# First group of a retention and FP4-linear kernel: next body's first k projection brought forward, ring loads from the staging area, second gate's transposes behind q

## The reference, cut to what matters

```python
xn = layernorm(x)                                  # x: (4, 1024, 1024)
q, k, v = heads(xn @ Wq + bq) * hd**-0.5, heads(xn @ Wk + bk), heads(xn @ Wv + bv)
ret = einsum('bhid,bhjd->bhij', q, k) * D          # D[i, j] = exp(decay * (i - j)) for i >= j, else 0
ret = ret / clip(abs(ret.sum(-1)), 1)
g = group_norm(einsum('bhij,bhjd->bhid', ret, v)) * gn_w + gn_b
attn = (silu(xn @ Wg + bg) * g) @ Wo + bo
ffn = fp4_quantized(xn) @ fp4_quantized(weight).T * scale + bias
return x + attn + ffn
```

## Time and profile before

| | before |
|---|---|
| median of 3 runs | 2137.29 us (2134.43 to 2142.41) |
| profiled execution, its time | 2142.48 us |
| its span | 2140.7 us |
| granted TensorE clock, mean | 0.991 |
| PE busy | 2080.3 us, 97% |
| DVE busy | 1541.7 us, 72% |
| ACT busy | 685.9 us, 32% |
| POOL busy | 640.0 us, 30% |

### The profile page before, as it was taken

The page is one execution under the profiler, slowest core; times in us unless marked ns, Lnnn a source line. Parts: engine busy times, 40 slices in busy tenths (PEclk is TensorE's granted clock), DMA queues, the critical chain, the costliest instruction groups (busy, mean ns, idle before and its releaser), DMA issues.

```text
span 2140.7 us, 51098 instructions
## 1 busy us (share of the span) xinstructions
PE 2080.3 (97%) x18098; PEld 1053.5 (49%) x18098; DVE 1541.7 (72%) x4375; ACT 685.9 (32%) x1318; POOL 640.0 (30%) x456
## 2 busy tenths in 40 slices
PE   5988899999999999999999999999999999999999
PEld 3444444455455454555555555454555454555444
DVE  7899898988889877566767556767656767656732
ACT  5756623332223233322323322323322322322300
POOL 1323232332233333223332223233223233223220
PEclk8999999999999999999999999999999999999999
DMA  8878634334343443323333323333323333223343
GB/s 317 282 253 265 218 98 138 108 109 136 100 127 108 137 128 94 102 83 109 124 103 93 103 84 109 122 103 94 103 85 107 122 103 95 103 86 106 122 153 117
DMA packets 181686, 275.61 MB, mean 129 GB/s; under 512 B 117344, under 2 KB 117472, under 8 KB 181344
## 3 DMA queue, kind: packets, MB, share of 16 engines
q1 hardware_dynamic: 181600, 274.48, 39.8%
HBM read 204.18 MB, written 40.89 MB: 114 GB/s over the span
## 4 chain that ended last, share of the span: by engine, by line
PE 86%; DVE 11%; DMA 2%; issue 1%; ACT 0%; SPq 0%; DVEq 0%; ACTq 0%
PE mm L1288 54%; PE mm L1223 10%; PE tp L1223 6%; PE mm L1232 4%; PE tp L1298 3%; PE four L1338 3%; PE four L1351 2%; PE tp L1326 1%; PE four L1311 1%; PE four L1232 1%; PE tp L1251 1%; DVE wo L929 1%; DMA res<-in_w_f 1%; DMA parts<-wo 1%; DVE state L1041 1%
## 5 line engine op out<-in xcount | busy, mean ns | idle before, releaser
L1288 PE MATMUL mm<-xnT,wring 128*128 128x512 f16 x6144 | 1365.8, 381 | 13.8 <-DVE wring L929 6.8
L1288 PEld LDWEIGHTS mm<-xnT,wring 128*128 128x128 f16 x6144 | 598.2, 98 | 710.3 <-issue 25.2
L695 ACT ACTIVATE work<-four,gs 128x64 f32<-128x64 f32 x512 | 158.1, 414 | 554.2 <-DVE gs L1068 554.2
L556 POOL TENSOR_TENSOR yT<-gn,gate 128x512 f32 (+1 forms) x64 | 84.2, 1315 | 800.6 <-ACT gn L706 800.6
L1223 PE MATMUL mm<-wo,yT 128*128 128x512 f16 x960 | 214.1, 380 | 0.1
L1055 DVE BATCH_NORM_STATS2 gst<-four 128x6 f32<-128x64 f32 x512 | 73.5, 216 | 195.0 <-PE four L1351 194.8
L539 POOL TENSOR_TENSOR qparts<-qT,qparts 128x512 f16<-128x512 f32 x64 | 77.0, 1203 | 363.2 <-ACT qT L664 363.1
L539 POOL TENSOR_TENSOR kparts<-kT,kparts 128x512 f16<-128x512 f32 x64 | 84.2, 1316 | 225.1 <-ACT kT L664 225.1
L1223 PEld LDWEIGHTS mm<-wo,yT 128*128 (+1 forms) x960 | 91.0, 98 | 108.3 <-issue 0.2
L1223 PE MATMUL tp<-wo,yT 128*128 128x512 f16 x576 | 128.2, 379 | 0.0
L662 ACT ACTIVATE qparts<-mm,consts,down 128x512 f16<-128x512 f32 x64 | 49.7, 776 | 213.2 <-PE mm L1288 213.2
(11 more groups left out here) (198 smaller groups left out, 2648.8 us busy)
## 6 DMA issues: line engine op xcount, KB each, us to landing
wring<-parts SPq DMA_DIRECT2D x252, 512.0 KB, 3.9
xt<-in_x SPq DMA_DIRECT2D x34, 512.0 KB, 3.6
out<-res SPq DMA_DIRECT2D x32, 512.0 KB, 3.0
parts<-wo SPq DMA_DIRECT2D x28, 512.0 KB, 5.6
res<-in_x SPq DMA_DIRECT2D x28, 512.0 KB, 3.5
ftile<-in_w_f SPq DMA_DIRECT2D x12, 512.0 KB, 4.4
parts<-wring SPq DMA_DIRECT2D x8, 512.0 KB, 6.8
probs<-in_x SPq DMA_DIRECT2D x5, 512.0 KB, 4.6
```

The costliest lines, as they stand in the source:

```text
L556: nc.gpsimd.tensor_tensor(hi, gn[:], gate[:, u], ALU.mult)
L695: last = nc.scalar.activation(work[:, c * P + h * HD:c * P + (h + 1) * HD], ao[h][:, c * VW:c * VW + HD], ACT.Identity, bias=gs[:, 1, g:g ...
L1288: last = MM(mm[n % 2][:], wring[:, n, wj, k, :], xnT[:, parity, xj, k, :], start=(j == 0), stop=(j == 3 * KT - 1))
```

## The change

In the first group only: PE does the k projection of the next body's first pair behind the second scores of this one, and ACT evacuates it there (`project` and `evacuate` have an argument `ahead`). `load_slice` reads the slice from `wo` instead of `parts` in all bodies but the last one's second half, and so waits for `lo_done` instead of `stored`; SP's calls of `load_slice(1, n)` are interleaved with the stores of the next batch, and the square that overwrites a slice of `wo` waits until the ring load has read it (`w_k` and so on). PE's `transpose_g(1, 1)` goes behind the q projection, and ACT's `affine(1, 1)` behind the evacuation of q. DVE does the second half of the quantization behind the first states in bodies 1 to 3, and `find_f_max` of the first tiles behind the second mask.

```diff
--- before.py
+++ after.py
@@ -371,10 +371,12 @@
                     w(f"mm{n % 2}_full", mm_use(u, n))
-                    if (phase, i, u) == (FIRST, 0, 0):
-                        sp.wait_ge(stored[n], 32)
-                        sp.wait_ge(lo_done, 4 + n + 1)
-                        src, dst = wo[:, :, 4 + n, :], wring[:, n].rearrange("p b k x -> p b (k x)")
+                    if phase == FIRST and (i, u) != (CH - 1, 1):
+                        b, c = i + u, 4 * (1 - u) + n
+                        if (i, u) == (0, 0):
+                            sp.wait_ge(stored[n], 32)
+                        sp.wait_ge(lo_done, SLICES * b + c + 1)
+                        src, dst = wo[:, :, c, :], wring[:, n].rearrange("p b k x -> p b (k x)")
                     else:
@@ -444,15 +446,17 @@
                         move_x_parts()
                         load_slice(0, 3)
+                    load_slice(1, 0)
+                    pass_on(i + 1, range(0, 1))
+                    load_slice(1, 1)
+                    pass_on(i + 1, range(1, 2))
                     w("xq_ready", 1)
                     move_x()
                     load_x(1)
-                    pass_on(i + 1, range(0, 2))
-                    load_slice(1, 0)
-                    load_slice(1, 1)
-                    pass_on(i + 1, range(2, 4))
                     load_slice(1, 2)
+                    pass_on(i + 1, range(2, 3))
                     load_slice(1, 3)
+                    pass_on(i + 1, range(3, 4))
                     pass_on(i + 1, range(4, 5))
                     load_fs(F_TILES[i][1])
@@ -617,8 +621,9 @@
                         act.wait_ge(stored[c], 16 * (b if c >= 4 else b + 1))
-                    if b == 1 and c >= 4:
-                        act.wait_ge(s["w_" + MATS[c - 4]], 16)
+                    loads = 2 * b - 1 if c >= 4 else 2 * b - 2
+                    if loads > 0:
+                        act.wait_ge(s["w_" + MATS[c % 4]], 16 * loads)
...
@@ -734,13 +741,15 @@
                 hi = lambda *slices: split_hi(i + 1, slices)
-                evacuate(0, 0)
+                if i == 0:
+                    evacuate(0, 0)
                 evacuate(0, 1)
                 if i:
-                    affine(1, 1)
                     square(i + 1, range(0, 4))
                 x_hi()
                 evacuate(0, 2)
+                if i:
+                    affine(1, 1)
                 copy_v(0)
@@ -760,6 +769,8 @@
                 evacuate(1, 3)
                 affine(0)
+                if i + 1 < CH:
+                    evacuate(0, 0, ahead=1)
                 normalize(1)
@@ -1096,8 +1107,6 @@
                     quantize_half(xt, 0)
-                    if i:
-                        quantize_half(xt, 1)
                     mask_scores(0)
@@ -1106,9 +1115,11 @@
                     scale_batch()
                     states(0)
                     split_lo(i + 1, range(0, 2))
-                    find_f_max(F_TILES[i][0])
+                    if i:
+                        quantize_half(xt, 1)
                     group_norm(0)
                     mask_scores(1)
+                    find_f_max(F_TILES[i][0])
                     split_lo(i + 1, range(2, 3))
                     states(1)
@@ -1354,10 +1366,10 @@
-                project(0, 0)
+                if phase != FIRST or i == 0:
+                    project(0, 0)
...
                 project(0, 1)
-                if phase != FIRST or i:
+                if phase != FIRST:
                     transpose_g(1, 1)
                 project(0, 2)
+                if phase == FIRST and i:
+                    transpose_g(1, 1)
                 transpose_kv(0, "v", vT, 1)
@@ -1388,6 +1403,8 @@
                 scores(1)
                 if phase == FIRST:
+                    if i + 1 < CH:
+                        project(0, 0, ahead=1)
                     state_increments(1)
```

More of the change, by code:

```diff
@@ L649, in pair, with evacuate @@
                     return ds(q * 2 + u, 1)
-                def evacuate(u, n):
+                def evacuate(u, n, ahead=0):
+                    w = waiter(act, phase, i + ahead)
+                    at_pair = ds((q + ahead) * 2 + u, 1)
                     use = mm_use(u, n)
@@ L662, in evacuate @@
                         nc.scalar.activation((kparts, None, qparts)[n][:, 0], mm[0][:], ACT.Identity,
-                                             bias=bias[:, n, pair(u)], scale=down[:, n, pair(u)])
+                                             bias=bias[:, n, at_pair], scale=down[:, n, at_pair])
                     nc.scalar.activation(dst, mm[n % 2][:], ACT.Silu if n == 3 else ACT.Identity,
-                                         bias=bias[:, n, pair(u)], scale=down[:, n, pair(u)])\
+                                         bias=bias[:, n, at_pair], scale=down[:, n, at_pair])\
                       .then_inc(s[f"mm{n % 2}_free"], 1)
@@ L1275, in body, with project @@
                     return
-                def project(u, n):
+                def project(u, n, ahead=0):
+                    w = waiter(pe, phase, i + ahead)
                     use = mm_use(u, n)
-                    if (phase, i, u) == (FIRST, 0, 0):
+                    if (phase, i + ahead, u) == (FIRST, 0, 0):
                         pe.wait_ge(lo_done, n + 1)
```

## The result

| | before | after |
|---|---|---|
| median | 2136.68 us of 4 runs (2134.43 to 2142.41) | 2186.95 us of 4 runs (2186.49 to 2188.52) |
| profiled execution, its span | 2142.48 us, 2140.7 us | 2186.86 us, 2185.1 us |

The change makes the kernel slower: ratio 1.0225, 95% interval 1.0205 to 1.0245. The forecast was 2174 us with a range of 2148 to 2194; the time lies in the range and 13 us above the forecast.

A forecast was written before the change was run, and what follows sets the result against it. DVE's chain was taken to bound the first group's bodies 1 to 3, with PE nearly full. Body losses 2 + 10.9 + 13.6 + 9.9 = 36.4 us on the 2137.3 us median gave 2174 us, range 2148 to 2194.

The forecast's parts named there:

- t: Time within a body, in us after DVE starts that body's layernorm.
- the two holds: ACT, bodies 1 to 3: first, affine waits behind x_hi, ending t = 7.9; second, square 7 awaits gate-slice load, t = 24.9.
- only the first hold: Rival: gate slice lands before ACT reaches square 7, so only late affine costs; 2150 us, chance 0.12.
- not slower: Rival: PE, not DVE, is late at a body's head, so late affine delays no one; 2124 us, chance 0.07.
- worse: Rival: gate slice takes twice as long and PE's clock falls in both pauses; about 2191 us, chance 0.09.
- the 4.2 taken: Ring's gate slice load on SP: lands 4.2 us after issue, at t = 24.9; the row used was an HBM load.
- the sum of 36.4: First group's added time over bodies 0 to 3: 2 + 10.9 + 13.6 + 9.9 = 36.4 us.
- without the 1.11 us wait: DVE, end of body 2: FFN weight tile priced at 1.2 us, its earlier 1.11 us wait taken as gone.
- The moved half, priced at 5.0: DVE, bodies 1 to 3: second quantize half behind the first states takes 5.0 us, delaying the first group norm.
- The projection behind the second pause: PE's second v projection after 7.4 us idling: 7.03 us instead of 5.3, bounds 5.3 and 8.6.
- DVE has the last word: First group, bodies 1 to 3: both engines nearly full, DVE sets the pace; a microsecond on its chain is worth a microsecond.
- PE's wait of 2.90 us: Body 2 before: PE stands 2.90 us before state increments until DVE masks the scores; counted as waiting the change removes.

The follow-up runs named there:

- Undoing the two holds: Changed kernel with affine(1, 1) and transpose_g(1, 1) put back and the ring's gate slot load ahead of the transposes of x: 2145.16 us, ratio 1.0034.
- one line: Changed kernel with SP's load of the ring's gate slot ahead of the transposes of x, affine(1, 1) staying behind x_hi: 2163.43 us, ratio 1.0115.
- taking 5.8 us of them away: Changed kernel with both affine/transpose_g and gate-load edits, plus the second FFN tile's load ahead of the ring's next q slice: 2143.5 us, ratio 1.0030.
- one pair of kernels: Kernel before with moved quantize half and find_f_max, without and with the second FFN tile's early load: 2143.72 us (1.0022) and 2144.78 us (1.0025).
- the DVE part alone: Kernel before with only the second quantize half behind the first states and find_f_max behind the second mask: 2143.72 us, ratio 1.0022.

## Why the prediction was right, and where it was off

**The side and the mechanism held.** `gn` ends at t = 7.8 (forecast 7.9), the second v projection starts at 27.0 (26.9), the first states at 34.6 (34.6), the first group norm at 46.3 (45.4), the second states at 55.1 (54.3). These times are of body 1. In body 2, on whose rows the forecast was worked out, the last four are 27.9, 36.4, 48.1 and 56.9, up to 2.7 us later than forecast. Undoing the two holds takes back 41.8 of 50.3 us: they are the cause of that part, shown by the runs. The rival "only the first hold" falls with the 10.86 us wait and with the 23.5 us that one line gives back; "not slower" falls with PE's 9.77; "worse" asked for a landing twice as long, and the square went on 3.3 us after the load's issue at 130.09, so the landing was no longer than the 4.2 taken. Its other half came true: PE was slower behind both pauses, not only behind the second. Its time, 2191, is nearer to the 2187 measured than the forecast is, but the 12 us that it put on the landing did not occur.

**The missing 13 us.** Two things. First, the base: I put the sum of 36.4 on the median, 2137.3, and the profiled execution of before, from which the bodies' lengths come, lay 5.2 us above it; after, profile and median agree. The difference of medians is therefore 50.3 and that of the two traces 44.4. There is no second trace of before, but 3.6 of the 5.2 us can be found in code that other kernels share with it. From the second group's first layernorm on all 14 kernels are the same and take 1857.6 to 1862.2 us, before 1861.6, about 2.0 above the median; and the kernel with only the later `affine`, the same up to body 1, comes to body 1 at 102.99 us, before at 104.55. Second, 8 us of the sum itself, 0.4 of it ahead of body 0 and the rest by body +3.4, +12.7, +16.9 and +11.0 for 2, 10.9, 13.6 and 9.9:

- *The weight tile was taken to be waited for no longer.* It was, for 0.96, 1.96 and 1.86 us in bodies 0 to 2: 4.8. The tile's load is the last in SP's list for a body, and it comes as late as everything else. The wrong step is the tile taken "without the 1.11 us wait". How much of the 4.8 would come back without these waits is open: with both holds undone, taking 5.8 us of them away gave 1.7.
- *The moved half, priced at 5.0, took 5.96* in body 2: two of its instructions fell beside POOL's split and decay of the second q (225.25 to 226.66 and 226.74 to 228.34).

```profile
224.95 0.69 DVE L851 TENSOR_TENSOR xa<-xa,xm 128x512 f32<-128x512 f32 x1
225.68 1.53 DVE L852 TENSOR_TENSOR xa<-xa,xm 128x512 f32<-128x512 f32 x1
227.24 1.65 DVE L853 TENSOR_TENSOR xq<-xa,qs 128x512 bf16<-128x512 f32 x1
```

- *The projection behind the second pause* took 6.83, 7.74 and 6.62 us; 7.03 was right on average. I gave no such price to the first pause, after which two projections took 12.57 us instead of 10.5. The first scores are 2.4 us late for it (t = 21.9, not 19.5), which the second hold covers in the changed kernel, but not where that is undone. That is part of why the first rival's 2150 was too low: with the second hold undone the kernel took 2163.

**"DVE has the last word"** is borne out only in part. Time added to DVE's list by the holds lengthened the bodies. But that a microsecond taken from the list "is worth a microsecond" did not hold: 8.0 of 9.8 us of tile waits came back in the layernorms of one pair of kernels, and 3.2 of 5.8 in another. And that PE's wait of 2.90 us costs nothing is not tested, since the DVE part alone only moved that wait to the second increments. "The added projection itself costs nothing while DVE is that late" holds in bodies 1 and 2 within about a microsecond; in body 0, where the forecast gave +2, taking it away gives 2.3 us back. The Trainium skill, SBUF — State Buffer, section "SBUF: two separate sides", names DVE instructions with two SBUF inputs beside a GpSimd instruction that reads SBUF as ones that block each other; the L841 and L842 rows above agree in the sign (0.69 against 1.53 and 1.64), and so do the L796 and L797 rows of the layernorm (0.25 and 0.16 against 1.16 and 1.21); no run here takes POOL's work away to settle it.

## What to carry to other kernels

On an engine that works in order, look at what stands behind an instruction before giving it a later input: here a multiply by two vectors and a square, 1 us each, held a PSUM bank, POOL and a ring slot, and cost 42 us. Where a load's source buffer is used again, the reuse waits for the load's landing, and so for all that stands ahead of it in the queue; putting that one load ahead gave half of the loss back. Price an edit in the kernel it will stand in: the later `affine` cost 7.5 us where DVE came late to the scores anyway and no square waited behind `x_lo`, and 16.6 where both had changed. And a wait taken out of an engine's list is won only if what follows can use the time: most of the 9.8 us of tile waits came back in the layernorm, which then ran beside POOL.

## What the runs showed of the hardware that was not expected

PE's pauses cost twice. After 9.77 us of idling the next 48 matmuls took 12.57 us, after 9.93 us 12.39, and without a pause 10.52. In body 1 of the changed kernel the granted clock was 0.55 in the first pause (106.60 to 116.30), 0.81 from there to the end of the two projections (116.31 to 129.75), 0.78 in the projection behind the second pause (135.34 to 142.17) and 1.00 in the next (144.19 to 149.53); these are means between the two levels, 0.5 (1.2 GHz) and 1.0 (2.4 GHz). And an instruction of DVE has no one price: the same L853 took 2.50, 1.65 and 0.69 us in one trace. The layernorm, the same rows each time, took 4.7 to 8.5 us in bodies 0 to 3 of the 14 traces, 4.7 where POOL had hardly any work beside it and 8.5 where `gate_y` ran through it.
